# Attention and mixture-of-experts layer: the normalised rows stored through GpSimd's queue, row by row to places in a list, in place of SyncE's block store

## The chip, the core and the metric

The kernel runs on one core of one Trainium2 chip. The metric is the device time of one execution, in microseconds. All times of the trace are microseconds from the start of the profiled span. Engines are named as in the profile: PE is TensorE (PEld its weight loads), DVE is VectorE, ACT is ScalarE, POOL is GpSimd, SP is SyncE. A trailing q (SPq) is the queue of an engine, where DMAs are issued.

## The reference, cut

The input is x of 32 x 256 x 128: 32 batches of 256 tokens with 128 features. The layer is attention with 16 heads of 8 features, a residual and a normalisation, and then a routed feed-forward layer with 8 experts, of which each token takes 2, again with a residual and a normalisation.

```python
qkv = x @ W_qkv.T + b_qkv                      # 16 heads, 8 features for q, k and v each
att = softmax(q @ k.T / sqrt(8)) @ v
x1 = layernorm(x + att @ W_out.T + b_out)      # the "normalised rows" of this document
scores = sigmoid(x1 @ gate_w.T)                # top 2 of 8 by scores + bias
r = score * x1
out_r = score * ((silu(r @ w1[e].T) * (r @ w3[e].T)) @ w2[e].T)   # for the 2 experts of each token
shared = (silu(x1 @ sw1.T) * (x1 @ sw3.T)) @ sw2.T
out = layernorm(x1 + shared + out_r summed over the token's 2 experts)
```

All is float32. q and k are split into three bfloat16 parts each, so that their product keeps its precision.

## The kernel before, in words

**First stage, attention.** A batch is 256 tokens: two tiles of 128 (NT is 2). The work is cut into slots (class Slot, from L155). In slot s each engine works on several batches at once, each at another step: load is batch s+5, proj s+4 (q and k computed and split), stack s+3 (the parts brought back from DRAM in stacked order), maxi s+2 (row maxima of the scores), neg s+1 (the maxima brought into the stack as two more rows), soft s (scores and exponentials), tail s-1, norm s-2 (residual, normalisation), gated s-3 (routing scores). The slots run from -4 to 34; slots 3 to 26 are a loop of four slots a turn (slots, L178). A step that has no batch (below 0 or over 31) is left out, so norm is live in slots 2 to 33, and proj in slots up to 27.

Each engine has its own instruction list, in order, and the lists meet at semaphores. There is no planner: the order within a slot is written out by hand.

**POOL in a slot** (L414): wait until the maxima of neg's batch are done (max_red), and write them as two bfloat16 parts into max_two (L425, L427). Then wait for var_eps from DVE and compute rstd (L432). Then wait until the transposes and the DRAM store of the last x1_new are done (x1_T, x1_kept, L435 and L436). Then x_bo, the residual with the output bias (L445), and x1_new, the normalised rows, in two instructions, one for each tile (L449). Then wait for q and k of proj's batch (qk_f, L454), and six subtractions which split them: L456 and L457 for q, the same for k, then the third parts in L459 and L461. SP's stores of these parts wait for the sixth (split_step). At the end the transposed rows are copied into x1T (L471), and the next slot begins with max_two. In slot 0 three long subtractions of the weights (L467) stand between the splits and the end.

**PE in a slot** (L722): 16 heads in pairs, for each pair the shifted scores of soft (L668) and the scores for the maxima of maxi (L681), and between the pairs, one by one, the small steps of the other batches: the gate and the output projection (L749, L756), the transposition of max_two (L769, which waits for max_lo_set, that is for L427), v (L783, which waits for DVE's max_rows, L1000), q and k (L793, L797), and the transpositions L812, L822 (of x1_new) and L831, with the products of probabilities and values (L696) between them. All these small steps share one bank, misc.

**DVE in a slot** (L944): a reduction for each head (L967), the residual and its statistics (L982 to L992), max_rows (L1000), and the steps on attention tokens (L1006, L1010). **ACT** has the exponentials (L537) and what leaves the bank misc: attT (L548), v_aug (L571), q and k (L586 to L591), x1T_new (L562), attc (L555).

**SP in a slot** (L312): the load of xT, then the wait for proj's parts in DRAM and the four stack loads (L329), the two loads of the maxima's rows (L335), the load of x (L341), then the store of x1_new, and then the wait for all six splits and the six stores of the parts (L361, L363). The store of the normalised rows is one block of 256 rows:

```python
if b.live:                                      # b = t.norm, L351
    sp.wait_ge(x1_set, b.count(2, 2))
    sp.dma_start(x1_dram[bass.ds(b.n * NT, NT), :, :].rearrange("i p c -> p i c"), x1_new[:]).then_inc(x1_kept, 16)
```

After the last slot SP waits until all stores have landed (L373).

**Second stage, experts.** 16 groups of 512 tokens. SP brings x1 back from x1_dram for the residual (L386), one load a group; the products read x1T in SBUF, not x1_dram. PE's groups begin when the last x1T copy is done (x1T_kept, L846).

Of the kernel before, what the change touches and what calls it, by code (L numbers as in the profile page):

```python
# [10 lines left out]
F32 = mybir.dt.float32  # L11
BF16 = mybir.dt.bfloat16
F32R = mybir.dt.float32r

P = 128
# [34 lines left out]
def attention_moe_layer(nc, x, xT, wqT, wkT, wvT, bq, bk, bv, woT, bo, gateT, ebias, rank, w1T, w3T, w2T, out):  # L50
    C, N = xT.shape
    B = 32
    T = N // B
    NT = T // P
# [4 lines left out]
    TILES = N // P  # L59
# [10 lines left out]
    with ExitStack() as ctx:  # L70
        def sb(name, shape, dt=F32):
            return ctx.enter_context(nc.sbuf_tensor(name, shape, dt))

        def sem(name):
            return ctx.enter_context(nc.semaphore(name))
# [4 lines left out]
        x1_dram = nc.dram_tensor("x1_dram", [TILES, P, C], F32, kind="Internal").ap()  # L80
# [25 lines left out]
        qf, kf, rq, rk = (sb(n, [P, T]) for n in ("qf", "kf", "rq", "rk"))  # L106
# [10 lines left out]
        stats, mv = sb("stats", [P, NT, 6]), sb("mv", [P, NT, 2])  # L117
        var_eps, rstd = sb("var_eps", [P, NT]), sb("rstd", [P, NT])
        x1_new, x1T_new = sb("x1_new", [P, NT, C]), sb("x1T_new", [P, T])

# [24 lines left out]
        x1_set, x1_kept, x1_T, x1T_set, x1T_kept = (sem(n) for n in ("x1_set", "x1_kept", "x1_T", "x1T_set", "x1T_kept"))  # L145
        gate_mm, logits_set = sem("gate_mm"), sem("logits_set")


# [142 lines left out]
        def _(sp):  # L291
# [20 lines left out]
            def slot(t):  # L312
                b = t.stack
# [5 lines left out]
                b = t.load  # L319
# [4 lines left out]
                b = t.stack  # L324
# [6 lines left out]
                b = t.neg  # L331
# [13 lines left out]
                if not b.looped and b.c == B - 1:  # L345
# [3 lines left out]
                    for e in range(E):  # L349
                        load_weight(0, e)  # L350
                if b.live:  # L351
                    sp.wait_ge(x1_set, b.count(2, 2))
                    sp.dma_start(x1_dram[bass.ds(b.n * NT, NT), :, :].rearrange("i p c -> p i c"), x1_new[:]).then_inc(x1_kept, 16)
                b = t.proj
# [17 lines left out]

            sp.wait_ge(x1_kept, 16 * B)  # L373

# [24 lines left out]
        def _(pool):  # L399
# [7 lines left out]
            pool.wait_ge(consts_set, 4)  # L407
            pool.tensor_copy(ident_bf[:], ident[:]).then_inc(consts_set, 1)

            def split_x(g, r):  # L410
# [3 lines left out]
            def slot(t):  # L414
# [14 lines left out]
                if b.live:  # L429

                    pool.wait_ge(eps_set, b.count(1, 1))
                    pool.tensor_tensor(rstd[:], var_eps[:], minus_half[:, 0:NT], ALU.pow).then_inc(rstd_set, 1)  # L432
                    pool.wait_ge(rstd_set, b.count(1, 1))
                    if b.later(1):
                        pool.wait_ge(x1_T, b.count(1, 0))  # L435
                        pool.wait_ge(x1_kept, b.count(16, 0))  # L436
                b = t.tail
# [8 lines left out]
                b = t.norm  # L446
                if b.live:
                    for i in range(NT):
                        pool.tensor_scalar(x1_new[:, i, :], res[:, i, :], mv[:, i, 0:1], rstd[:, i:i + 1],  # L449
                                           ALU.subtract, ALU.mult).then_inc(x1_set, 1)  # L450
                b = t.proj
                if b.live:

                    pool.wait_ge(qk_f, b.count(4, 4))  # L454
                    for full, rest, parts in ((qf, rq, q_parts[b.ring % 2]), (kf, rk, k_parts[b.ring % 2])):
                        pool.tensor_tensor(rest[:], full[:], parts[:, 0, :], ALU.subtract).then_inc(split_step, 1)  # L456
                        pool.tensor_tensor(parts[:, 1, :], full[:], parts[:, 0, :], ALU.subtract).then_inc(split_step, 1)  # L457
                    pool.wait_ge(split_step, b.count(6, 2))
                    pool.tensor_tensor(q_parts[b.ring % 2][:, 2, :], rq[:], q_parts[b.ring % 2][:, 1, :], ALU.subtract).then_inc(split_step, 1)  # L459
# [703 lines left out]
```

## Time and profile before

| | |
|---|---|
| median of 3 runs | 914.75 us (913.73 to 917.01) |
| the profiled execution | 911.17 us |
| its span, first to last instruction | 909.4 us |
| granted TensorE clock over the span | 0.978 of full speed |
| busy: PE, DVE, ACT, POOL | 88%, 80%, 64%, 55% |
| DMA | 108.83 MB, mean 120 GB/s |
| DMAs issued by POOL | none |
| stores of the normalised rows | 32, of 128 KB each, from SP's queue |

The durations all come from the profiled execution, and its own time is the 911.17 us beside the span of 909.4; the runs' median is 3.6 us above it. Instructions that only issue a DMA, wait or branch are not counted as busy. In a timeline row the first number is the start, the second the length, "x2" a merged run of two instructions, and the bracket at the end the idle time of the engine before it and what ended it.

### The profile page before, as it was taken

The numbers are of one execution on the slowest core, as the hardware profiler recorded it, in microseconds if no ns is written. First come the engines' busy times: TensorE is split into PE (matmuls) and PEld (weight loads), VectorE is DVE, ScalarE is ACT, GpSimd is POOL, SyncE is SP. The second block draws the span as 40 slices with busy tenths as digits, with TensorE's granted clock in tenths as the row PEclk, the third lists the DMA queues.
The fourth block names the chain that finished last, engine by engine and source line by source line (L and its number), as shares of the span: only waits on it lengthen the run. The fifth ranks groups of instructions, "written<-read, shape, count | busy, mean of one in ns | idle before, by whom it ended". The sixth has DMA issues, their size and how long they took to land.

```text
span 909.4 us, 21516 instructions
## 1 busy us (share of the span) xinstructions
PE 800.3 (88%) x6228; PEld 468.5 (52%) x6228; DVE 723.6 (80%) x1430; ACT 586.5 (64%) x1192; POOL 500.7 (55%) x620
## 2 busy tenths in 40 slices
PE   2678999999999999999998778999999999999994
PEld 1233444544444454444444356766666666666662
DVE  4665888888888888888888448888888887888886
ACT  1165878787787878778787535555555565555652
POOL 2344455554555555455543426766666666666664
PEclk9996999999999999999999969999999999999997
DMA  5553546546464554645451073344544444444440
GB/s 145 150 139 84 155 121 145 149 114 165 126 143 129 133 149 117 165 123 143 125 129 32 15 173 81 84 119 117 123 116 116 110 121 120 116 115 116 124 113 28
DMA packets 201642, 108.83 MB, mean 120 GB/s; under 512 B 10496, under 2 KB 201088, under 8 KB 201600
## 3 DMA queue, kind: packets, MB, share of 16 engines
q1 hardware_dynamic: 200048, 105.88, 44.4%
q10 hardware_dynamic: 1552, 2.44, 0.9%
q8 instruction: 20, 0.33, 0.2%
q14 instruction: 22, 0.18, 0.1%
HBM read 73.94 MB, written 33.82 MB: 118 GB/s over the span
## 4 chain that ended last, share of the span: by engine, by line
PE 43%; DVE 19%; issue 18%; POOL 10%; DMA 3%; ACT 3%; DVEq 1%; SPq 1%; POOLq 0%; ACTq 0%
PE bank L696 8%; PE bank L668 6%; DVE negmax L967 4%; PE bank L681 4%; POOL place L489 4%; PE bank L703 3%; PE bank L704 3%; PE bank L705 3%; DVE k_stack L1034 3%; PE bank L793 3%; PE bank L783 2%; PE bank L797 2%; PE bank L857 2%; POOL rstd L498 2%; DMA probs<-route_dram 2%
## 5 line engine op out<-in xcount | busy, mean ns | idle before, releaser
L967 DVE TENSOR_REDUCE negmax<-bank 128x2 f32<-128x512 f32 x512 | 330.8, 685 | 75.3 <-PE bank L681 71.1
L537 ACT ACTIVATE probs<-bank 128x512 f32<-128x512 f32 x512 | 281.1, 598 | 99.5 <-PE bank L668 96.2
L681 PE MATMUL bank<-k_stack,q_stack 48*128 48x256 bf16 x1024 | 165.9, 286 | 8.0 <-DMA k_stack<-k_parts_dram 4.1
L668 PE MATMUL bank<-q_stack,k_stack 50*128 50x256 bf16 x1024 | 159.7, 277 | 4.2 <-ACT probs L537 4.1
L696 PE MATMUL bank<-probs,v_aug 128*32 128x256 f32 x2048 | 161.2, 395 | 0.5 <-ACT attT L548 0.4
L703 PE MATMUL bank<-x_hi,hi_w 128*128 128x512 f32 x288 | 138.3, 480 | 10.6 <-DVE k_stack L1034 8.0
L668 PEld LDWEIGHTS bank<-q_stack,k_stack 50*128 50x128 bf16 x1024 | 75.9, 96 | 104.2 <-ACT probs L537 75.6
L1024 DVE TENSOR_TENSOR k_stack<-bank,probs 128x512 f32<-128x512 f32 x128 | 87.6, 685 | 43.4 <-DMA probs<-route_dram 21.3
L704 PE MATMUL bank<-x_hi,lo_w 128*128 128x512 f32 x288 | 115.4, 401 | 0.0
L705 PE MATMUL bank<-x_lo,hi_w 128*128 128x512 f32 x288 | 115.3, 400 | 0.0
L489 POOL TENSOR_TENSOR k_stack<-k_stack,probs 128x512 f32<-128x512 f32 x48 | 62.1, 1294 | 80.8 <-DVE k_stack L1034 73.1
L640 ACT ACTIVATE q_stack<-k_stack 128x512 f32<-128x512 f32 x128 | 79.4, 620 | 36.4 <-DVE k_stack L1024 35.8
L618 ACT ACTIVATE probs<-probs 128x512 f32<-128x512 f32 x128 | 79.3, 620 | 12.0 <-DMA probs<-route_dram 11.3
L681 PEld LDWEIGHTS bank<-k_stack,q_stack 48*128 48x128 bf16 x1024 | 72.7, 97 | 26.6 <-DVE negmax L967 13.6
L456 POOL TENSOR_TENSOR rq<-qf,q_parts 128x256 f32<-128x256 f32 x32 | 21.5, 673 | 116.6 <-ACT k_parts L591 116.6
L432 POOL TENSOR_TENSOR rstd<-var_eps,minus_half 128x2 f32<-128x2 f32 x32 | 23.2, 726 | 109.7 <-DVE var_eps L992 109.7
L703 PEld LDWEIGHTS bank<-x_hi,hi_w 128*128 128x128 f32 x288 | 55.2, 192 | 50.8 <-DVE k_stack L1034 18.8
L696 PEld LDWEIGHTS bank<-probs,v_aug 128*32 128x32 f32 x2048 | 50.3, 109 | 44.4 <-issue 29.4
L627 ACT ACTIVATE hs_hi<-k_stack 128x512 fp32r<-128x512 f32 x48 | 30.1, 627 | 56.9 <-POOL k_stack L489 56.9
L704 PEld LDWEIGHTS bank<-x_hi,lo_w 128*128 128x128 f32 x288 | 55.4, 192 | 18.7 <-issue 9.7
L1034 DVE TENSOR_TENSOR k_stack<-bank,q_stack 128x512 f32<-128x512 f32 x96 | 63.9, 678 | 0.8 <-ACT q_stack L640 0.7
L489 POOL TENSOR_TENSOR k_stack<-q_stack,probs 128x512 f32<-128x512 f32 x32 | 41.3, 1290 | 38.3 <-DVE q_stack L1034 27.9
(111 smaller groups left out, 1405.6 us busy)
## 6 DMA issues: line engine op xcount, KB each, us to landing
probs<-route_dram SPq DMA_DIRECT2D x128, 256.0 KB, 5.9
q_stack<-q_parts_dram SPq DMA_DIRECT2D x64, 192.0 KB, 3.3
k_stack<-k_parts_dram SPq DMA_DIRECT2D x64, 192.0 KB, 4.1
q_parts_dram<-q_parts SPq DMA_DIRECT2D x32, 192.0 KB, 2.0
k_parts_dram<-k_parts SPq DMA_DIRECT2D x32, 192.0 KB, 2.1
xT_sb<-xT SPq DMA_DIRECT2D x32, 128.0 KB, 2.1
q_parts_dram<-q_parts SPq DMA_DIRECT2D x32, 128.0 KB, 1.9
k_parts_dram<-k_parts SPq DMA_DIRECT2D x32, 128.0 KB, 1.9
```

The lines of the kernel that those rows point to most:

```text
L489: pool.tensor_tensor(hid_s[n % DEPTH], hid[n % DEPTH], weight2_b[n - 1], ALU.mult).then_inc(hids_set, 1)
L537: nc.scalar.activation(probs[h][:], score_ps[BANK[h]][:].rearrange("p (j t) -> p j t", j=NT), ACT.Exp).then_inc(exp_done, 1)
L640: nc.scalar.activation(act[n % DEPTH], gated[n % DEPTH] if n else up1_ps[0][:], ACT.Silu).then_inc(act_set, 1)
L668: mm = pe.matmul(score_ps[BANK[h]][:, j * T:(j + 1) * T], k_stack[b.ring][first:last, h // 2, j * P:(j + 1) * P], q_stack[b.ring][first:la ...
L681: mm = pe.matmul(max_ps[BANK[h]][:, i * T:(i + 1) * T], q_stack[b.ring][first:last, h // 2, i * P:(i + 1) * P], k_stack[b.ring][first:last ...
L696: mm = pe.matmul(av_ps[32 * hh:32 * hh + 32, half * T:(half + 1) * T], v_aug[b.ring][:, 2 * j + half, u, hh, :], probs[4 * quad + hh][:, j ...
L703: pe.matmul(ps[:], w_hi[m][:, n, :], hi[:], start=start, stop=False)
L704: pe.matmul(ps[:], w_lo[m][:, n, :], hi[:], start=False, stop=False)
L705: return pe.matmul(ps[:], w_hi[m][:, n, :], lo[:], start=False, stop=stop)
L967: nc.vector.tensor_reduce(negmax[b.ring % 2][:, :, column], max_ps[BANK[h]][:].rearrange("p (i s) -> p i s", i=NT), AX_X, ALU.max, negate= ...
L1024: nc.vector.tensor_tensor(gated[n % DEPTH], up1_ps[n % DEPTH][:], weight_b[e], ALU.mult).then_inc(gated_set, 1)
L1034: nc.vector.tensor_tensor(hid[n % DEPTH], up3_ps[n % DEPTH][:], act[n % DEPTH], ALU.mult).then_inc(hid_set, 1)
```

## The change

The store of the normalised rows leaves SP's list. POOL gets a table of row numbers, row_ids, written once at the start (row p of tile n has the number 128 n + p). In each slot with a norm batch it copies the two columns of this batch to rows_now, ahead of x1_new. Then it waits for x1_set and rows_set, and issues two indirect DMAs, one for each tile of 128 rows: each of the 128 partitions is written to the row of x1_dram that its entry of rows_now names. In slots in which proj is live too (2 to 27) the two are issued after the first two split operations, those of q; in the others (28 to 33) at once. Each DMA adds 16 to x1_kept, so the waits on it count 32 a batch, not 16.

```diff
@@ SyncE, slot
-                if b.live:
-                    sp.wait_ge(x1_set, b.count(2, 2))
-                    sp.dma_start(x1_dram[bass.ds(b.n * NT, NT), :, :].rearrange("i p c -> p i c"), x1_new[:]).then_inc(x1_kept, 16)
@@ SyncE, after the slots
-            sp.wait_ge(x1_kept, 16 * B)
+            sp.wait_ge(x1_kept, 16 * NT * B)
@@ GpSimd, start
             pool.tensor_copy(ident_bf[:], ident[:]).then_inc(consts_set, 1)
+            pool.iota(row_ids[:], [[P, TILES]], base=0, channel_multiplier=1).then_inc(ids_set, 1)
+            pool.wait_ge(ids_set, 1)
@@ GpSimd, slot
                     if b.later(1):
                         pool.wait_ge(x1_T, b.count(1, 0))
-                        pool.wait_ge(x1_kept, b.count(16, 0))
+                        pool.wait_ge(x1_kept, b.count(16 * NT, 0))
...
                 b = t.norm
                 if b.live:
+                    pool.tensor_copy(rows_now[:], row_ids[:, bass.ds(b.n * NT, NT)]).then_inc(rows_set, 1)
                     for i in range(NT):
                         pool.tensor_scalar(x1_new[:, i, :], res[:, i, :], mv[:, i, 0:1], rstd[:, i:i + 1],
                                            ALU.subtract, ALU.mult).then_inc(x1_set, 1)
+                def keep_rows(b):
+
+                    for i in range(NT):
+                        pool.indirect_dma_start(x1_dram.rearrange("a p c -> (a p) c"), bass.IndirectOffsetOnAxis(ap=rows_now[:, i:i + 1], axis=0),
+                                                x1_new[:, i, :], None).then_inc(x1_kept, 16)
+
+                if t.norm.live:
+                    pool.wait_ge(x1_set, t.norm.count(2, 2))
+                    pool.wait_ge(rows_set, t.norm.count(1, 1))
+                if t.norm.live and not t.proj.live:
+                    keep_rows(t.norm)
                 b = t.proj
                 if b.live:
...
                     for full, rest, parts in ((qf, rq, q_parts[b.ring % 2]), (kf, rk, k_parts[b.ring % 2])):
                         pool.tensor_tensor(rest[:], full[:], parts[:, 0, :], ALU.subtract).then_inc(split_step, 1)
                         pool.tensor_tensor(parts[:, 1, :], full[:], parts[:, 0, :], ALU.subtract).then_inc(split_step, 1)
+                        if full is qf and t.norm.live:
+                            keep_rows(t.norm)
```

The rest of the diff declares row_ids, rows_now, the type U32 and the semaphores ids_set and rows_set.

## Rows read from the trace of the kernel before

**Rows 1.** The page, busy time of each engine, share of the span, instructions.

```profile
PE 800.3 (88%) x6228; PEld 468.5 (52%) x6228; DVE 723.6 (80%) x1430; ACT 586.5 (64%) x1192; POOL 500.7 (55%) x620
```

**Rows 2.** Stretches: length, busy time of PE, PEld, DVE, ACT, POOL; clock, DMA share, GB/s.

```profile
333.98:348.43 14.45, 13.50 (x158) 6.99 (x154) 12.44 (x27) 11.50 (x26) 7.66 (x13) 1.00 0.50 137
```

**Rows 3.** Waits from 300 to 500: who waited for whom, total, times, longest.

```profile
POOL rstd L432 <- DVE var_eps L992: 46.2, 14, 3.4
POOL rq L456 <- ACT k_parts L591: 29.2, 12, 2.7
POOL max_two L425 <- DVE negmax L967: 10.4, 14, 1.5
```

**Rows 4.** Timeline of POOL in one slot of the loop: start, length, instruction.

```profile
344.18 0.68 POOL L456 TENSOR_TENSOR rq<-qf,q_parts 128x256 f32<-128x256 f32 x1 [2.30 <-ACT k_parts L591]
...
347.94 0.39 POOL L471 COPY x1T<-x1T_new 128x256 f32 x1
349.00 0.25 POOL L425 TENSOR_TENSOR max_two<-negmax,ones 128x32 bf16<-128x32 f32 x1 [0.67 <-DVE negmax L967]
349.33 0.24 POOL L427 TENSOR_TENSOR max_two<-negmax,max_two 128x32 bf16<-128x32 f32 x1
...
353.90 0.72 POOL L445 TENSOR_TENSOR x_bo<-x_sb,bo_sb 128x256 f32<-128x256 f32 x1 [0.25 <-POOL rstd L432]
```

**Rows 5.** Timeline of PE in the slot behind it.

```profile
351.42 0.23 PE L769 MATMUL bank<-ident_bf,max_two 128*32 128x128 bf16 x1
...
353.81 0.35 PE L783 MATMUL bank<-wv_sb,xT_sb 128*128 128x128 f32 x1 [0.69 <-DVE max_rows L1000]
```

**Rows 6.** All instructions of L353: issue in ns (least, median, most), and landing in us.

```profile
L353 SPq DMA_DIRECT2D x_dram<-x_new x32: 373/425/496, 96.6 to 532.9; - x32
...
DMA to landing us min/median/max: 1.8/2.3/4.2
```

**Rows 7.** Groups of POOL's instructions by shape: busy us, mean ns, idle before.

```profile
L449 POOL TENSOR_SCALAR x_new<-res,mv,rstd 128x128 f32<-128x128 f32 x64 | 51.2, 807 | 0.1
...
L427 POOL TENSOR_TENSOR max_two<-negmax,max_two 128x32 bf16<-128x32 f32 x32 | 7.8, 245 | 2.5
```

**Rows 8.** Timelines of SP and PE; the page's DMA issues (KB each, us to landing).

```profile
353.11 0.98 SPq L329 DMA_DIRECT2D k_stack<-k_parts_dram  x2
...
363.02 0.28 PE L668 MATMUL bank<-q_stack,k_stack 50*128 50x256 bf16 x1
...
k_stack<-k_parts_dram SPq DMA_DIRECT2D x64, 192.0 KB, 4.1
```

**Rows 9.** Timelines of POOL and PE in slot 0, in which POOL splits the weights.

```profile
65.89 7.78 POOL L467 TENSOR_TENSOR lo_w<-x1T,hi_w 128x1152 fp32r<-128x1152 f32 x3
...
73.96 0.24 POOL L427 TENSOR_TENSOR max_two<-negmax,max_two 128x32 bf16<-128x32 f32 x1
...
74.26 0.29 PE L769 MATMUL bank<-ident_bf,max_two 128*32 128x128 bf16 x1 [2.31 <-POOL max_two L427]
```

**Rows 10.** Timeline of ACT in the loop slot; and a wait of PE, from 300 to 500.

```profile
353.01 0.60 ACT L537 ACTIVATE probs<-bank 128x512 f32<-128x512 f32 x1 [0.62 <-PE bank L668]
...
354.53 0.28 ACT L571 ACTIVATE v_aug<-bank 128x128 f32<-128x128 f32 x1
...
PEld bank L793 <- ACT v_aug L571: 2.7, 10, 0.3
```

**Rows 11.** Timeline of slot 33 and the start of the second stage.

```profile
531.28 1.57 POOL L449 TENSOR_SCALAR x_new<-res,mv,rstd 128x128 f32<-128x128 f32 x2
...
534.08 0.40 POOL L471 COPY x1T<-x1T_new 128x256 f32<-128x256 f32 x1 [1.23 <-ACT x1T_new L562]
...
535.40 0.77 PE L703 MATMUL bank<-x_hi,hi_w 128*128 128x512 f32 x1 [0.31 <-issue]
```

**Rows 12.** Timeline of POOL in slot 31; and the group of DVE's reductions, 300 to 500.

```profile
508.03 1.12 POOL L445 TENSOR_TENSOR x_bo<-x_sb,bo_sb 128x256 f32<-128x256 f32 x1
...
L967 DVE TENSOR_REDUCE negmax<-bank 128x2 f32<-128x512 f32 x215 | 139.1, 685 | 20.5 <-PE bank L681 18.8
```

More of the change, by code:

```diff
@@ L12 @@
 BF16 = mybir.dt.bfloat16
+U32 = mybir.dt.uint32
 F32R = mybir.dt.float32r
@@ L118, in attention_moe_layer @@
         var_eps, rstd = sb("var_eps", [P, NT]), sb("rstd", [P, NT])
+        row_ids, rows_now = sb("row_ids", [P, TILES], U32), sb("rows_now", [P, NT], U32)
         x1_new, x1T_new = sb("x1_new", [P, NT, C]), sb("x1T_new", [P, T])
@@ L146, in attention_moe_layer @@
         gate_mm, logits_set = sem("gate_mm"), sem("logits_set")
+        ids_set, rows_set = sem("ids_set"), sem("rows_set")
         BANK = [h % 3 for h in range(H - 1)] + [1]
```

## The prediction

> **What bounds the kernel now.** I read the page first for the share of each engine: TensorE is busy 88% of the span, GpSimd 55% [rows 1]. The mean hides two stages. The change touches only the first, attention, which runs in "slots", one batch further per slot. The table by stretch for one slot in the loop shows 14.45 us, of which PE is busy 13.50, DVE 12.44, ACT 11.50 and POOL 7.66 [rows 2]. So PE's in-order stream, paced by hand-offs with DVE and ACT, sets the slot, and POOL has 6.8 us to spare. But POOL's spare time does not lie where the change needs it. The list of waits shows where it lies: before rstd (46.2 us over 14 slots, 3.3 each) and before the first split operation (29.2 over 12, 2.4 each); only 10.4 over 14, 0.7 each, lies before max_two [rows 3].
>
> The timeline of POOL in one slot gives the stretch that matters [rows 4]: the six split operations start at 344.18 when ACT has delivered k_parts, the copy of x1T runs from 347.94 to 348.34, then POOL waits 0.67 us and runs max_two at 349.00 and 349.33, until 349.57. Behind them PE transposes max_two (L769) at 351.42 without a wait [rows 5]. PE's queue is in order, so what makes L769 late makes everything behind it late.
>
> **What the change removes.** SyncE's wait for x1_new and one issue of 0.42 us per slot; the store lands after 2.3 us [rows 6]. SyncE begins the next parts stores only when POOL's last split is done, at about 348, so it idles there in either case: worth nothing. The 128 KB still go to DRAM in 512-byte rows, so the DMA engines carry the same load.
>
> **What it adds, at nothing.** An iota and its wait at the start come after ident_bf, and POOL's next work there waits for ACT anyway. The copy rows_now stands before x1_new, ahead of the 2.4 us idle before the splits [rows 3]; if that cover were gone it would cost the duration of a tiny operation, about 0.1 to 0.25 us [rows 7]. The wait for x1_set and rows_set has behind it the wait for the split's inputs, which ends later. The rows leave at about 345.5 to 348 instead of 342. The next batch's x1_new waits for their landing, in front of x_bo at 353.90 [rows 4]; with a landing of 2.3 us they are down by about 350.5, 3.4 us early.
>
> **What it adds, at a price: two DMAs issued by POOL itself.** They stand between the second and the third split operation, in the 26 slots in which a batch is normalised and another is projected (slots 2 to 27). Everything behind them on POOL moves by D, the time that the two take: k's splits, the third parts, the x1T copy, and max_two. Who waits for these?
> - SyncE's parts stores, then the stack loads behind them. The stores start at about 348, the last of the stack loads follows at about 353.6 and lands 4.1 us later, at 357.7. PE needs them with the next slot at 363.02 [rows 8]. That is over 5 us of room.
> - The x1T copy is wanted by ACT one slot later.
> - max_two: free as long as D is under POOL's idle 0.67 plus PE's distance, 351.42 less 349.57, less some 0.06 for the signal (in slot 0 POOL ended at 74.20 and PE started at 74.26 [rows 9]). That is 0.67 + 1.85 - 0.06 = 2.46; since the weight load before L769 starts 0.05 earlier, I take 2.4.
> Over 2.4 each us costs nearly a us. PE does idle 0.69 us in front of L783 [rows 5], but I do not count it as cover: late scores make ACT's exponential at 353.01 late, which is followed without a gap by attT, another exponential and v_aug at 354.53, and PE already waits for v_aug in 10 of 14 slots [rows 10]. The trace has one trial of this by itself. In slot 0 POOL ran 7.78 us of weight splits ahead of max_two, and PE stood 2.31 us at L769, with DVE and ACT starved behind it [rows 9].
>
> **The price of one DMA issued by POOL.** No row has one. Lower bound: SyncE issues the whole store in 0.42 us [rows 6]; POOL would hardly be faster for half of it. Upper bound: POOL's longest instruction, 7.78/3 = 2.59 us [rows 9]. Between them I go by the nearest thing, POOL's own cost per step. A tiny operation takes 0.245 us, x1_new's 128 steps 0.807 [rows 7], thus 4.4 ns a step. A list of 128 rows needs an address for the read and one for the write: 256 steps, 1.12 us. With 0.245 that is about 1.36 us, D = 2.7. Ends: D = 0.85 and D = 5.2.
>
> The Trainium skill has a price of its own: "SBUF — State Buffer" (A bandwidth-pool intuition that's wrong) gives about 620 ns for a DMA that GpSimd issues when nothing disturbs it. By that D would be 1.24, all of it would hide, and the sum would be that of the first rival; no row here shows such a DMA, and the page does not say that it goes by a list.
>
> **The end of the stage.** In slots 28 to 33 the DMAs stand right behind x1_new, ahead of the x1T copy. In the last one x1_new ends at 532.85 and the copy starts at 534.08, while PE starts the second stage at 535.40 [rows 11]. With D = 2.7 the copy ends at 532.9 + 2.7 + 0.4 = 536.0, and PE starts at 536.1: 0.7 us late, once. rows_now before x1_new, which is on the chain in the last three slots, adds about 0.1 each. Together 1.0.
>
> **Sum.** 26 x (2.7 - 2.4) = 7.8, and 1.0: 8.8 us. The profiled execution took 911.17 us (span 909.4), so 920.0 by its own time. It was 3.6 below the median of the runs, 914.75; on that scale the forecast is 923.5. A measurement of this kernel tells about 0.3%, 2.7 us, from no change.
>
> **Rivals.**
> - **Not slower: the two issues are short.** The point of decision is D = 2.4 to 2.5, 1.2 us per DMA, and my price of 1.36 lies close above it. Below it max_two is never late, and only about 0.5 us at the end of the stage stays: 915.2. For it: SyncE's 0.42. Against it: POOL is slow per step. Chance 0.42.
> - **POOL is held until the rows have landed**, as with the 2.3 us of the store now [rows 6]: D = 4.6, 26 x 2.2 = 57 and about 3 at the end, 975. Against it: the program asks for no such wait, SyncE's issues return long before landing. Chance 0.04.
> - **DVE keeps POOL from writing its lists.** In slot 31 x_bo took 1.12 us beside DVE's all-SBUF operations, against 0.73 in the loop [rows 4, 12]; in the loop DVE's reductions read PSUM and POOL's operations keep their pace. If each DMA had to wait out one reduction of 0.685 us [rows 12], D would be 2.7 + 1.4 = 4.1, 26 x 1.7 = 44 and 2 at the end: 961. Chance 0.04. The Trainium skill, "SBUF — State Buffer" (SBUF: two separate sides), has this as a rule: while VectorE holds the shared pair of ports, GpSimd cannot write descriptors; slot 31 agrees in kind, the loop shows nothing of it.
> - **Faster**, since SyncE's queue is shorter by 0.42 us a slot and the rows stay out of the stack loads' way: 26 x 0.42 = 11 at most, 904. Nothing waits for these loads, so 0.02.
> - The forecast's own case, D from 2.5 to about 4: 0.48.
>
> **How the numbers follow.** The forecast's case runs from 917 (D = 2.5) to 914.75 + 26 x 1.6 + 2 = 958 (D = 4.0), and D over 3.7 is unlikely in it: 914.75 + 26 x 1.3 + 1.5 = 950. The low end takes in the first rival, 913. So 913 to 950 holds about 0.85. Slower: 0.48 + 0.04 + 0.04 = 0.56; within 0.3%: 0.42; faster: 0.02. The likeliest case alone: 917 to 950.
>
> **What would show it.** Right: POOL's gap between its second and third split grows from nothing to about 2.7 us; SyncE's first parts store starts that much later; a wait of PE for max_two at L769 in each loop slot of about 0.3 us, and a slot of about 14.75 us. Wrong: a gap under 2.4 with slots of 14.45 us (first rival); a gap of 4.6 that ends with the landing (second); gaps that jump with DVE's operations (third). If the gap is 2.7 and the slot still 14.45, then PE's 0.69 us before L783 was cover after all.

## The result, and the profile after

| | before | after |
|---|---|---|
| median | 914.31 us (913.73 to 917.01, 4 runs) | 949.29 us (944.5 to 952.29, 4 runs) |
| ratio | | 1.0372, 95% interval 1.0317 to 1.0427 |
| profiled execution, its span | 911.17, 909.4 us | 952.29, 950.5 us |

The change costs 35 us. The forecast was 923.5 with a range to 950, so the sign and the range hold, but the 8.8 us of its sum explain a quarter of it. Among the executions of the later kernels two lie far from the rest of their group and enter no ratio, 949.62 us of the kernel apart at a clock of 0.80 and 1646.41 us of the kernel twoplain; without them the medians given for these two would be 918.23 and 915.55. The page of the kernel after (its lines are those of the kernel before plus some 16):

```profile
PE 820.5 (86%) x6228; PEld 472.6 (50%) x6228; DVE 722.0 (76%) x1430; ACT 585.9 (62%) x1192; POOL 573.3 (60%) x717
...
L983 DVE TENSOR_REDUCE negmax<-bank 128x2 f32<-128x512 f32 x512 | 328.0, 685 | 102.9 <-PE bank L697 99.4
L553 ACT ACTIVATE probs<-bank 128x512 f32<-128x512 f32 x512 | 284.1, 601 | 136.9 <-PE bank L684 133.2
...
L457 POOL DMA_INDIRECT x_dram<-x_new,rows_now x64 | 67.3, 1052 | 15.9 <-issue 14.2
```

The two middle groups, DVE's reductions and ACT's exponentials, read so on the page of the kernel before:

```profile
L967 DVE TENSOR_REDUCE negmax<-bank 128x2 f32<-128x512 f32 x512 | 330.8, 685 | 75.3 <-PE bank L681 71.1
L537 ACT ACTIVATE probs<-bank 128x512 f32<-128x512 f32 x512 | 281.1, 598 | 99.5 <-PE bank L668 96.2
```

Against [rows 1], POOL works 73 us more, 67.3 of them the list DMAs (L457; a list DMA is one that goes by a list of rows). PE, too, shows 20 us more for the same matmuls. DVE and ACT idle 28 and 37 us more for scores of PE: 99.4 and 133.2 us, against 71.1 and 96.2.

The timeline of POOL in one slot of the kernel after, the counterpart of [rows 4]:

```profile
352.28 0.68 POOL L471 TENSOR_TENSOR q_parts<-qf,q_parts 128x256 bf16<-128x256 f32 x1
353.12 1.11 POOL L457 DMA_INDIRECT x_dram<-x_new,rows_now  x1 [0.17 <-issue]
354.54 0.96 POOL L457 DMA_INDIRECT x_dram<-x_new,rows_now  x1 [0.30 <-issue]
355.53 0.68 POOL L470 TENSOR_TENSOR rk<-kf,k_parts 128x256 f32<-128x256 f32 x1
...
358.39 0.24 POOL L427 TENSOR_TENSOR max_two<-negmax,ones 128x32 bf16<-128x32 f32 x1
358.71 0.24 POOL L429 TENSOR_TENSOR max_two<-negmax,max_two 128x32 bf16<-128x32 f32 x1
```

The second and the third split start 3.25 us apart, where 0.63 is their distance with nothing between: D = 2.62, forecast 2.7. SP's first store of the parts follows at 358.11, right behind the last split. So far the forecast. But PE does not stand at max_two's transposition:

```profile
359.82 0.23 PE L785 MATMUL bank<-ident_bf,max_two 128*32 128x128 bf16 x1
```

No idle time in brackets, unlike L769 of slot 0 in [rows 9]; the list of waits from 300 to 520 has no wait of PE for max_two at all. And yet the slots are a whole us longer, some more. The table by stretch, from max_two to max_two (length, busy PE, PEld, DVE, ACT, POOL, granted clock, DMA share, GB/s), beside the 14.45 of [rows 2]:

```profile
342.99:358.39 15.40, 13.83 (x156) 7.00 (x155) 12.33 (x27) 11.38 (x25) 9.88 (x17) 1.00 0.51 129
...
373.78:389.29 15.51, 13.93 (x156) 7.10 (x156) 12.42 (x27) 11.47 (x26) 9.87 (x17) 1.00 0.49 128
389.29:406.15 16.86, 15.36 (x157) 7.61 (x156) 12.33 (x27) 11.55 (x25) 9.88 (x17) 0.90 0.46 118
```

Over 25 slots of the loop the two kernels compare so (before, then after):

```profile
103.76:464.70 360.94, 337.20 (x3851) 174.52 (x3851) 310.16 (x651) 287.20 (x626) 191.45 (x325) 1.00 0.53 137
```

```profile
103.98:499.99 396.01, 356.48 (x3841) 178.90 (x3836) 307.39 (x649) 286.55 (x625) 247.04 (x402) 0.97 0.49 125
```

That is 35.1 us in 25 slots, 1.40 each: practically the whole loss. (The spans differ by 41.1, since the profiled execution of before lies 3.1 below its median and that of after 3.0 above its own.) Where in the slot are they? These are the timelines of PE, ACT and DVE of the kernel after during the second list DMA (354.54 to 355.50):

```profile
354.68 0.27 PE L684 MATMUL bank<-q_stack,k_stack 50*128 50x256 bf16 x1
...
355.10 0.44 PE L847 MATMUL bank<-ident,att_tok 128*128 128x128 f32 x2
355.47 0.64 PE L712 MATMUL bank<-probs,v_aug 128*32 128x256 f32 x8
356.04 0.28 PE L684 MATMUL bank<-q_stack,k_stack 50*128 50x256 bf16 x1
...
357.06 0.28 PE L684 MATMUL bank<-q_stack,k_stack 50*128 50x256 bf16 x1 [0.63 <-ACT probs L553]
```

```profile
355.92 1.09 ACT L553 ACTIVATE probs<-bank 128x512 f32<-128x512 f32 x2 [1.35 <-PE bank L684]
```

```profile
355.95 2.49 DVE L983 TENSOR_REDUCE negmax<-bank 128x2 f32<-128x512 f32 x4 [1.26 <-PE bank L697]
```

PE's matmuls run on schedule. The first head's scores are computed by 354.68 + 0.27 = 354.95 (ends of PE are modelled), but ACT begins with them at 355.92, 0.97 us later, and DVE at 355.95, both just behind the end of the list DMA. Only then does the lateness come back to PE: at 357.06 it waits for a bank that ACT has not yet read. I call this a hold: ACT and DVE see late what PE has finished.

The trace also has a list of the moments at which each semaphore was incremented, and it shows which side is late. PE's increments for the scores whose matmuls end at 354.95 and 355.17 come at 355.90 and 355.98, and ACT starts at 355.92. So PE's increments come late, and ACT takes them up at once. In the kernel before, no increment of PE in the loop comes more than 0.14 us behind the modelled end of its matmul. Those of ACT, DVE and POOL come within 0.02 us of the ends of their instructions, before and after.

The other part is the clock. In the slot of 16.86 us:

```profile
387.00:388.00 1.00, 0.36 (x7) 0.08 (x5) 1.00 (x2) 1.00 (x3) 1.00 (x3) 1.00 0.14 45
...
389.00:390.00 1.00, 1.00 (x10) 0.78 (x13) 0.35 (x1) 0.26 (x1) 0.78 (x3) 0.66 0.04 13
390.00:391.00 1.00, 1.00 (x10) 0.18 (x8) 0.82 (x4) 0.00 (x0) 0.00 (x0) 0.50 1.12 373
391.00:392.00 1.00, 1.00 (x13) 0.47 (x13) 0.69 (x3) 0.50 (x2) 0.00 (x0) 0.50 0.84 271
392.00:393.00 1.00, 1.00 (x17) 0.76 (x13) 0.97 (x5) 0.59 (x2) 0.33 (x1) 0.63 0.44 130
```

The granted clock is 0.50, 1.2 of 2.4 GHz, for over 2 us, soon after the stall (in the us from 387 PE was busy 0.36 us, still at a clock of 1.00), and the slot is 1.5 us longer than its neighbours. Eight of the 25 slots last 16.8 to 16.95 with a clock of 0.90; in the kernel before the mean over the stretch is 1.00. So of 35.1 us some 12 (8 x 1.5) are the clock, and the rest, 23, is 0.9 a slot.

### The profile page after: what moved, and what is told of

Same layout as the page of the kernel before. It is cut to its first block, busy times and chain, and to the rows that moved or that the text cites. A ratio compares the mean times of both kernels' runs of the same rounds, so it can differ in the third digit from the quotient of the medians.

```text
span 950.5 us, 21602 instructions
## 1 busy us (share of the span) xinstructions
PE 820.5 (86%) x6228; PEld 472.6 (50%) x6228; DVE 722.0 (76%) x1430; ACT 585.9 (62%) x1192; POOL 573.3 (60%) x717
## 4 chain that ended last, share of the span: by engine, by line
PE 47%; DVE 15%; issue 14%; POOL 10%; DMA 6%; ACT 4%; DVEq 1%; SPq 1%; POOLq 0%; ACTq 0%
PE bank L712 10%; PE bank L684 6%; PE bank L697 6%; DMA probs<-route_dram 4%; DVE negmax L983 4%; PE bank L719 4%; PE bank L720 3%; PE bank L721 3%; POOL place L505 3%; DVE k_stack L1050 3%; PE bank L809 2%; PE bank L873 2%; PE bank L813 2%; POOL rstd L514 2%; PE bank L772 2%
## 5 line engine op out<-in xcount | busy, mean ns | idle before, releaser
L983 DVE TENSOR_REDUCE negmax<-bank 128x2 f32<-128x512 f32 x512 | 328.0, 685 | 102.9 <-PE bank L697 99.4
L553 ACT ACTIVATE probs<-bank 128x512 f32<-128x512 f32 x512 | 284.1, 601 | 136.9 <-PE bank L684 133.2
L684 PE MATMUL bank<-q_stack,k_stack 50*128 50x256 bf16 x1024 | 170.7, 282 | 16.3 <-ACT probs L553 16.3
L697 PE MATMUL bank<-k_stack,q_stack 48*128 48x256 bf16 x1024 | 170.8, 289 | 11.2 <-DVE negmax L983 7.6
L712 PE MATMUL bank<-probs,v_aug 128*32 128x256 f32 x2048 | 168.7, 410 | 0.5 <-ACT attT L564 0.4
L457 POOL DMA_INDIRECT x_dram<-x_new,rows_now x64 | 67.3, 1052 | 15.9 <-issue 14.2
L712 PEld LDWEIGHTS bank<-probs,v_aug 128*32 128x32 f32 x2048 | 53.2, 112 | 45.5 <-issue 30.7
```

What stands on the lines that cost most here:

```text
L553: nc.scalar.activation(probs[h][:], score_ps[BANK[h]][:].rearrange("p (j t) -> p j t", j=NT), ACT.Exp).then_inc(exp_done, 1)
L684: mm = pe.matmul(score_ps[BANK[h]][:, j * T:(j + 1) * T], k_stack[b.ring][first:last, h // 2, j * P:(j + 1) * P], q_stack[b.ring][first:la ...
L697: mm = pe.matmul(max_ps[BANK[h]][:, i * T:(i + 1) * T], q_stack[b.ring][first:last, h // 2, i * P:(i + 1) * P], k_stack[b.ring][first:last ...
L712: mm = pe.matmul(av_ps[32 * hh:32 * hh + 32, half * T:(half + 1) * T], v_aug[b.ring][:, 2 * j + half, u, hh, :], probs[4 * quad + hh][:, j ...
L983: nc.vector.tensor_reduce(negmax[b.ring % 2][:, :, column], max_ps[BANK[h]][:].rearrange("p (i s) -> p i s", i=NT), AX_X, ALU.max, negate= ...
```

## Experiments

Three suspects: POOL's later work coming late (theory A, the forecast's own step); signals held by a DMA that POOL issues (theory B); and, in the later batches, what it takes for a hold. The runs of the kernel before that a batch shares are given with it.

### First batch: the delay alone, and one condition less (before: 915.28 us)

**fill.** The kernel before, its store left with SP, and four unread subtractions of POOL where the list DMAs would be.

```diff
+                def fill():
+                    for n in range(4):
+                        pool.wait_ge(fill_set, t.norm.count(4, n))
+                        pool.tensor_tensor(spin[0][:], x1_new[:], x1_new[:], ALU.subtract).then_inc(fill_set, 1)
```

> The kernel before, with SyncE's block store kept. POOL does four subtractions of 128x256, which nobody reads, at the place where the change has its two DMAs: about 2.7 us of plain work a slot and no DMA from POOL. Theory A (what costs is that POOL's later work comes 2.6 us later): about the time of the changed kernel, 940 to 955. Theory B (what costs is that signals of PE to DVE and ACT are held back while POOL writes its lists; delay by itself has 2.4 us of cover): loop slots of 14.45 to 14.9 us, 915 to 926 in all.

Measured 919.88 us, ratio 1.0050 (1.0029 to 1.0072). The same delay costs 4.6 us, not 35. A slot of it:

```profile
336.96:351.51 14.55, 13.57 (x157) 6.97 (x158) 12.38 (x27) 11.45 (x25) 10.03 (x19) 1.00 0.47 136
```

0.10 us over 14.45. (The slots of the kernel before run from 14.34 to 14.54 us, 14.44 in the mean.) Theory A carries about an eighth of the loss.

**early.** The kernel after with both list DMAs right behind x1_new, before the wait for the splits' inputs. A tiny subtraction, which the kernel after does not have, stands ahead of them.

```diff
+                    pool.wait_ge(tiny_set, t.norm.count(1, 0))
+                    pool.tensor_tensor(tiny[:], minus_half[:, 0:1], minus_half[:, 1:2], ALU.subtract).then_inc(tiny_set, 1)
-                if t.norm.live and not t.proj.live:
+                if t.norm.live:
                     keep_rows(t.norm)
...
-                        if full is qf and t.norm.live:
-                            keep_rows(t.norm)
```

> The changed kernel with both DMAs right behind x1_new in every slot, ahead of the wait for q and k, where POOL had 2.3 us of idle time (a tiny subtraction carries the wait ahead of them). Theory A: only 0.4 us of delay is left, max_two is in time, slots of 14.45 us, 914 to 917. Theory B: the signals are held all the same, about 2.8 us earlier in the slot, and PE's partners stand as before: slots of 15.0 to 15.6, 930 to 955.

Measured 917.91 us, ratio 1.0033 (1.0005 to 1.0062), slots of 14.34 to 14.54, which add up to the 360.9 us of the kernel before. The same two DMAs, as close behind each other:

```profile
355.34 1.11 POOL L458 DMA_INDIRECT x_dram<-x_new,rows_now  x1 [0.16 <-issue]
356.75 0.96 POOL L458 DMA_INDIRECT x_dram<-x_new,rows_now  x1 [0.30 <-issue]
357.74 0.69 POOL L473 TENSOR_TENSOR rq<-qf,q_parts 128x256 f32<-128x256 f32 x1
```

DVE idles 69.5 us for PE in this kernel, ACT 95.4, no more than before: no hold.

**plain.** One ordinary DMA for both tiles from POOL's queue, at the place of the two.

```diff
-                    for i in range(NT):
-                        pool.indirect_dma_start(...rows_now[:, i:i + 1]..., x1_new[:, i, :], None).then_inc(x1_kept, 16)
+                    pool.dma_start(x1_dram[bass.ds(b.n * NT, NT), :, :].rearrange("i p c -> p i c"), x1_new[:]).then_inc(x1_kept, 16)
```

> The changed kernel with one plain DMA of all 256 rows from POOL in place of the two with a list, at the same place. Theory A: POOL is away for about 1 to 1.3 us, under the 2.4 of cover, 914 to 917. Theory B, if any DMA whose descriptors POOL writes holds signals back: one hold of up to 0.9 us, slots of 14.6 to 15.4, 918 to 940. Theory B, if only the DMAs with a list do: 914 to 917.

Measured 914.08 us, ratio 0.9997 (0.9975 to 1.0019).

**onetile.** A list DMA for the first tile only, at its place; SP stores the second.

> The changed kernel with the list DMA for the first tile alone; SyncE stores the second tile. Theory A: D is 1.3, all covered, 914 to 917. Theory B: one hold in place of two; the first of the two in the changed kernel fell where few signals were due, and the second was the one seen to cost, so 915 to 930, with a hold to be seen about 0.4 to 1.4 us behind the start of the DMA.

Measured 914.82 us, ratio 0.9998 (0.9971 to 1.0025).

So B falls in its plain form. Neither a plain DMA from POOL nor one list DMA at this place is enough, nor is the pair at the place of early.

### Second batch: which pair? (before: 914.43 us)

**second.** The second tile's list DMA at its place, the first one replaced by two subtractions, with SP storing that tile.

> The second tile's list DMA stays where the changed kernel has it; the first tile's is replaced by two unread GpSimd subtractions (2 x 0.67 us), and SyncE stores the first tile. Theory P (the hold comes from a list DMA that is being issued at that moment of the slot, about 2 us behind the second split, whatever ran before it): signals of TensorE are held as in the changed kernel, slots of 15.4, so 26 x 0.94 = 24 us and more over before: 940 or more. Theory C (it takes two list DMAs close behind each other, the second issued while the first is landing): no held signal, slots of 14.45 to 14.55, 914 to 919 as with the one-tile kernel and the filled one.

Measured 922.80 us, ratio 1.0093 (1.0064 to 1.0123), slots of 14.52 to 14.58 as in the filled kernel. The long hold that P forecast is not there, so the moment alone does not make it. But there is a short one, against C, which forecast none. In each of the 25 slots PE's increment for the second head's scores comes 0.48 to 0.56 us late, and ACT starts on them 0.17 us late:

```profile
336.30 1.26 ACT L564 ACTIVATE probs<-bank 128x512 f32<-128x512 f32 x2 [0.42 <-PE bank L695]
```

The two exponentials take 1.26 us here, 1.09 in the kernel before. This does not lengthen the slots beyond the filled kernel's. Slots of 0.1 us more make 2.5 us of the 8.4 over before; the rest lies outside the loop's slots and stays unexplained.

**apart.** Both list DMAs, the second only behind the splits of k.

```diff
-                        if full is qf and t.norm.live:
-                            keep_rows(t.norm)
+                        if t.norm.live:
+                            keep_rows(t.norm, [0] if full is qf else [1])
```

> Both list DMAs, but the second only behind the two split operations of k, 1.4 us of GpSimd work later. Theory C (two close behind each other): no hold, 914 to 920. Theory P (the moment in the slot): the second is issued 1.4 us later than in the changed kernel, behind the last scores' signal, so no hold either, or one of another size (the values' signal); 914 to 930. A third, N (two list DMAs in this part of the slot, wherever they stand): held, 940 to 952.

Measured 918.66 us, ratio 1.0050 (1.0029 to 1.0070), slots of 14.46 to 14.49. As many DMAs, as late a max_two, and no hold that costs a slot anything: N falls. Short holds remain, though C forecast none: in 20 of the 25 slots an increment of PE comes 0.26 to 0.46 us late.

**twoplain.** Two DMAs without a list, one for each tile, at the place of the two with one.

> Two GpSimd DMAs of one tile each without a list, at the place of the two with one. If the list matters (its issue of 1.0 us each, against 0.83 for both tiles in one plain DMA): no hold, slots of 14.45 to 14.5, 914 to 917. If the number of GpSimd DMAs in a row is what counts: held signals, slots over 15, over 930.

Measured 915.79 us, ratio 1.0014 (0.9993 to 1.0035). Nothing is held, so it takes lists. The groups of instructions have these DMAs at 598 ns each, where those with a list take 1052.

**late.** The pair unbroken, but behind the splits of k.

> Both list DMAs one behind the other, but behind the splits of k, so 1.4 us later in the slot than in the changed kernel. Theory C (close behind each other is enough): held signals again, now those of 1.4 us later, slots over 15, over 930. Theory P (the moment): the first of the two is now issued where the changed kernel has its second, so by P it is held as well, slots of about 15.4, 940 or more. If neither (the moment of the second alone counts, together with a first before it): no hold, 914 to 920.

Measured 932.14 us, ratio 1.0198 (1.0166 to 1.0230), slots of 14.72 to 15.41. The hold is back, and this time it starts earlier against the DMAs, and another consumer of PE shows it too:

```profile
342.60 0.27 PE L697 MATMUL bank<-k_stack,q_stack 48*128 48x256 bf16 x1
...
342.68 1.27 ACT L553 ACTIVATE probs<-bank 128x512 f32<-128x512 f32 x2 [0.42 <-PE bank L684]
...
342.80 0.44 PE L847 MATMUL bank<-ident,att_tok 128*128 128x128 f32 x2
...
343.49 0.96 POOL L457 DMA_INDIRECT x_dram<-x_new,rows_now  x1 [0.30 <-issue]
...
344.00 0.09 PEld L684 LDWEIGHTS bank<-q_stack,k_stack 50*128 50x128 bf16 x1 [0.15 <-ACT probs L553]
...
344.06 0.69 DVE L983 TENSOR_REDUCE negmax<-bank 128x2 f32<-128x512 f32 x1 [0.66 <-PE bank L697]
...
344.79 0.47 ACT L571 ACTIVATE attc<-bank,bv_sb 128x256 f32<-128x256 f32 x1 [0.84 <-remote]
```

PE's transposition for attc starts at 342.80; ACT reads it at 344.79, 0.34 behind the end of the second DMA. The second head's scores, ready by 342.87, are reduced by DVE from 344.06 on, in the middle of that DMA. So a hold need not last until the list DMA is through. By the list of increments, three held ones of PE come at 343.33, 344.04 and 344.77, one about every 0.7 us. In the other direction nothing is late: ACT's exponentials end at 342.68 + 1.27 = 343.95, and PE goes on at 344.00. This fits C in its main point: the pair makes the long hold, its place the size.

### Third batch: landing, and two more places (before: 914.73 us)

**landed.** The pair at its place, but POOL waits for the first to land before it issues the second.

```diff
+                        if i:
+                            pool.wait_ge(x1_kept, b.count(16 * NT, 16))
+                            pool.tensor_tensor(tiny[:], minus_half[:, 0:1], minus_half[:, 1:2], ALU.subtract).then_inc(tiny_set, 1)
```

> Both list DMAs at the place of the changed kernel, but GpSimd waits for the first tile's landing (its 16 increments come 2.2 us after its start) and a tiny subtraction carries that wait, before it issues the second. Theory O (TensorE's signals are held while a second list DMA is issued over the landing of a first): no hold; GpSimd's later work comes about 0.9 us later still than in the changed kernel, so D is 3.5 to 3.7, which costs 26 x 0.9 at most: 915 to 940, and by the filled kernel's rate (0.1 us of a slot for D = 2.65) rather 918 to 935. Theory S (two list DMAs between the splits of q and k hold the signals, landed or not): 945 or more.

Measured 968.3 us, ratio 1.0572 (1.0493 to 1.0651), far outside both expectations. But nearly nothing is held (one increment of PE is 0.47 to 0.48 us late in 3 of the 25 slots, none over 0.22 in the others). The timelines show POOL first, then DVE during the second DMA, then PE:

```profile
350.19 1.11 POOL L462 DMA_INDIRECT x_dram<-x_new,rows_now  x1 [0.17 <-issue]
352.65 0.19 POOL L461 TENSOR_TENSOR tiny<-minus_half 128x1 f32<-128x1 f32 x1 [1.34 <-DMA x_dram<-x_new,rows_now]
352.99 1.00 POOL L462 DMA_INDIRECT x_dram<-x_new,rows_now  x1 [0.15 <-issue]
354.02 0.68 POOL L475 TENSOR_TENSOR rk<-kf,k_parts 128x256 f32<-128x256 f32 x1
```

```profile
353.58 1.29 DVE L988 TENSOR_REDUCE negmax<-bank 128x2 f32<-128x512 f32 x2 [0.19 <-PE bank L702]
...
357.50 0.23 PE L790 MATMUL bank<-ident_bf,max_two 128*32 128x128 bf16 x1 [1.47 <-POOL max_two L430]
```

DVE takes the scores in the middle of the DMA. What costs here is the forecast's mechanism in full: q_parts started at 349.35, so D = 354.02 - 349.35 - 0.63 = 4.04, and PE stands 1.47 us at max_two. The slot:

```profile
340.95:356.88 15.93, 13.54 (x154) 6.98 (x154) 12.45 (x27) 11.45 (x26) 10.10 (x18) 1.00 0.46 125
```

1.49 over before. My expectation took the rate of the filled kernel, whose D ends near the edge of the cover; beyond it each us costs a us. 26 x 1.49 = 39. Of the other 15, some 6 went to five slots of 17.1 early in the loop, all five with a clock of 0.90, and some 5 to the first two slots behind the weight splits (16.85 and 19.41, in the kernel before 15.48 and 14.33).

**onesplit.** The pair behind the first split of q, 0.68 us earlier.

> Both list DMAs behind the first split of q, 0.68 us earlier in the slot than in the changed kernel (the one placed 1.4 us later held signals for a shorter while: 932; the one some 7 us earlier held none: 918). Theory O (back to back is enough, what it costs depends on which of TensorE's signals fall into the second one's issue): held signals, slots over 14.6, 920 to 952. If neither, and GpSimd's later work is simply late: 917 to 922.

Measured 930.76 us, ratio 1.0157 (1.0099 to 1.0215), most slots of 14.9, the hold is there. (Against the splits the pair of early stands 3.9 us ahead of its place in the kernel after, not some 7 as this expectation says.)

**tail.** The pair behind all six splits.

> Both list DMAs behind all six splits, before the copy of x1T_new: 2.7 us of GpSimd's time before max_two as before, but SyncE's stores of the parts are no later than in the kernel before. Theory O: TensorE's signals of the last scores and of the output projection fall into the second one's issue and are held, slots over 14.6, 920 to 945. If the splits right behind the pair are needed for a hold: max_two is late as in the filled kernel, slots of 14.55, 918 to 922.

Measured 935.0 us, ratio 1.0228 (1.0173 to 1.0282), slots of 15.06 and 15.40. Both places have the hold, and a clock of 1.00 in all their longer slots. In the tail kernel PE's weight loads also wait for max_two, up to 1.0 us, so its loss is not the hold alone.

### Last run: the semaphore (before: 914.15 us)

**twosems.** The kernel after, in every place and order, but the second DMA counts on a semaphore of its own. The waits ask for both.

```diff
-                                                x1_new[:, i, :], None).then_inc(x1_kept, 16)
+                                                x1_new[:, i, :], None).then_inc(x1_kept_b if i else x1_kept, 16)
```

> The changed kernel, but each of the two list DMAs counts on a semaphore of its own. It tells whether the hold hangs on the first one's 16 increments coming to a semaphore that the second one, just being issued, counts on too. Theory O (the issue of the second over the data and increments of the first, whatever they count on): nothing changes, slots of 15.4 and more, 944 to 953 as the changed kernel. If it is the shared semaphore: no hold, 917 to 921 as the filled kernel.

Measured 918.18 us, ratio 1.0048 (1.0023 to 1.0073). I had thought this the less likely outcome. 31 of the 35 us are gone. Its page, a slot, and the timelines of POOL, ACT, PE's weight loads and DVE:

```profile
L985 DVE TENSOR_REDUCE negmax<-bank 128x2 f32<-128x512 f32 x512 | 330.8, 685 | 75.4 <-PE bank L699 71.2
L555 ACT ACTIVATE probs<-bank 128x512 f32<-128x512 f32 x512 | 282.0, 603 | 103.6 <-PE bank L686 98.9
```

```profile
336.13:350.64 14.51, 13.57 (x160) 6.97 (x158) 12.40 (x27) 11.44 (x25) 9.87 (x18) 1.00 0.48 137
```

```profile
345.38 1.11 POOL L459 DMA_INDIRECT x_dram<-x_new,rows_now  x1 [0.17 <-issue]
346.79 0.96 POOL L459 DMA_INDIRECT x_dram<-x_new,rows_now  x1 [0.30 <-issue]
```

```profile
347.24 1.09 ACT L555 ACTIVATE probs<-bank 128x512 f32<-128x512 f32 x2 [0.36 <-PE bank L686]
```

```profile
347.28 1.29 DVE L985 TENSOR_REDUCE negmax<-bank 128x2 f32<-128x512 f32 x2 [0.32 <-PE bank L699]
```

```profile
351.25 0.09 PEld L787 LDWEIGHTS bank<-ident_bf,max_two 128*32 128x32 bf16 x1 [0.32 <-POOL max_two L430]
```

The DMAs have the very durations of the kernel after, in the same place; but ACT and DVE begin at 347.24 and 347.28, in the middle of the second one. DVE idles 28 us less for PE than in the kernel after, ACT 34 less.

**All kernels beside each other.** For each of the 25 slots of the loop I took the increment of PE that comes latest behind the modelled end of its matmul. Where several are held at once this gives the least that the delay can be. The last column counts the increments by DMAs that are missing from the trace's list, of the 10320 or, in the kernels before, fill and plain, 9808 that the program makes.

| kernel | us | latest increment of PE, us | slots with one over 0.25 us | missing from the list |
|---|---|---|---|---|
| before, fill, plain, twoplain | 914 to 920 | 0.14 | 0 | 0 |
| onetile | 914.82 | 0.14 | 0 | 17 |
| twosems | 918.18 | 0.13 | 0 | 94 |
| early | 917.91 | 0.14 | 0 | 186 |
| landed | 968.3 | 0.48 | 3 | 464 |
| apart | 918.66 | 0.46 | 20 | 649 |
| second | 922.80 | 0.56 | 25 | 91 |
| onesplit | 930.76 | 1.24 | 25 | 992 |
| after | 949.29 | 1.36 | 25 | 534 |
| late | 932.14 | 1.58 | 25 | 440 |
| tail | 935.0 | 1.76 | 25 | 1226 |

The time follows only in part, since it also matters which signals are late, and when PE needs their answer.

## Why the forecast was right, and what it missed

- **The change's placement and D.** Right: two issues of 1.11 and 0.96 us and 0.47 between and before them, D = 2.62 against 2.7. The way to it, POOL's cost of 4.4 ns per step, was not tested, since no run has a list of another length; a plain DMA grows by 0.23 us from 128 to 256 rows, 1.8 ns a row. 620 ns, the price that "SBUF — State Buffer" of the Trainium skill gives for an undisturbed DMA from GpSimd, is near what the plain ones took (598 ns for 128 rows), and a list costs 0.45 more.
- **The cover of 2.4.** Somewhat small. From three kernels in whose slots next to nothing is held, D less what the slot grew: the filled one 2.65 - 0.10, two semaphores 2.61 - 0.06, landed 4.04 - 1.49, thus 2.55 each time. The forecast let a late weight load count in full; PE's load waits 0.32 us for max_two in the kernel with two semaphores, its matmul not at all. The sign "a wait of about 0.3 us" thus shows in that kernel, in the load; in the kernel after it is absent, and its slots are of 15.4 and 16.9, not of 14.75. So 26 x (2.62 - 2.55) = 2 instead of 7.8. The delay in all is the 4.0 us of the kernel with two semaphores; the other 2 lie outside the loop's slots and are as large as the scatter of single executions, so they are not assigned.
- **"Who waits for these?"** This is the step that failed. The forecast looked only for work that depends on POOL's instructions. The missing 31 us are with engines that wait for nothing of POOL: ACT and DVE get PE's signals 0.97 us late, and of the 35.1 us that the 25 slots lose, some 23 are this and some 12 the clock that follows. (The delay of POOL's work alone, with two semaphores, costs these slots 1.7 us.) No row of the kernel before could have shown it, since it has no such DMA. The range bounded D alone, and no rival had a cost in an engine that waits for nothing of POOL.
- **The rivals.** "Not slower" fails by the D it asks for, though its time, 915.2, is closer to what the delay costs than the forecast's. "Held until landing": POOL goes on at 355.53, and the second DMA's increments come from 356.60 on. "DVE keeps POOL from writing": the issues take 1.11 and 0.96 in slot after slot beside DVE's reductions; that rule is not seen in the loop. At the end of the stage some take 1.34 beside DVE's SBUF work; what holds them there was not tried.
- **The clock.** Not foreseen: in the kernel after, a stall of PE of about a us is followed by 2 us at 1.2 GHz in 8 of 25 slots, a second cost of 1.5 us each.
- By luck, the time fell inside the range: 949.3, with 950 its end.

What is settled: the delay of POOL's work alone costs 4 to 5 us (fill, twosems), and what is late beyond it are PE's increments. Long holds, with increments up to 1.2 to 1.8 us late, show in the four kernels with two list DMAs one right behind the other on one semaphore among or behind the splits (after, late, onesplit, tail). At the place of the kernel after they need the common semaphore (twosems has none). Short holds need no such pair: the single list DMA of second has them in every slot, and apart in 20 of 25.

What stays open: why the early kernel, with the pair and the common semaphore, has none. It differs in its place in PE's order and by a tiny subtraction, and no run tells the two apart. Nor is it known why the one list DMA of second holds something and that of onetile, which POOL issues 1.3 us earlier behind the splits of q, nothing. And it is open whether the hold belongs to the chip alone or to its recording: each timed execution was recorded. The answer for all instructions of a line ends with the DMAs' landing time where their increments are whole in the record; for the list DMA in the kernel with two semaphores it is

```profile
L459 POOL DMA_INDIRECT x_dram<-x_new,rows_now x64: 954/1112/1352, 98.6 to 537.8; - x64
...
DMA to landing us min/median/max: 2.2/2.4/8.0
```

The second of these lines is absent for the kernel after, late, onesplit and tail, all those with a long hold, and for apart. Of the 1024 increments that x1_kept gets in each of these kernels, the list has 659, 646, 652, 597 and 995; in early and landed it has all 1024. By the table above, increments of DMAs are missing in every kernel with list DMAs and in none without. So list DMAs go with gaps in the record, with or without a hold, and the recording stands as an untested rival for the cause. I have no mechanism for either.

## What to carry to other kernels

Two list DMAs issued one right behind the other from GpSimd, on one semaphore, can delay engines that have nothing to do with them. Give each its own semaphore, put other work between them, or issue them where the queue would idle; here each of the three brought some 31 us back (918.2, 918.7 and 917.9 against 949.3). Whether they would do so in a run that is not recorded, nothing here shows. When a DMA moves onto a compute engine's queue, look for its price not only behind it on that queue but in the idle time "<- PE" of all others. And a cover measured in the trace ends sharply: 2.6 us of delay cost 4 to 5 us in all, 4.04 us cost 54, of which 39 are PE's wait for max_two.

No version beats the kernel before. The plain DMA from POOL's queue (0.9997) and the one-tile kernel (0.9998) equal it.

## What the runs showed of the hardware that was not expected

- A list DMA of 128 rows takes POOL 1.11 us. The second one of a slot takes less: 0.96 right behind the first, 0.98 with two subtractions between them (apart), 1.00 behind the first one's landing (landed). Without a list it is 0.60, and 0.83 for 256 rows in one. It lands 2.4 us after its issue (median), like SP's store of both tiles in 2.3 [rows 6].
- The hold: for scores that PE has computed at 354.95 its increment comes at 355.90. Only PE's increments are held; ACT's, DVE's and POOL's come within 0.02 us in the kernels before, after, early, second, apart, late, landed, onesplit, tail and twosems. The long hold vanishes with a second semaphore. A list DMA alone on its semaphore can hold too, for 0.5 us (second).
- Eight of the 25 slots of the kernel after had TensorE's clock at its lower level for some 2 us; none of 25 in the kernel before. In landed, where PE waits 1.47 us a slot and next to nothing is held, five slots in a row have a mean clock of 0.90. In late, onesplit and tail all 25 stay at 1.00, though increments are held up to 1.76 us.
